# V projected in a phase of its own ahead of the attention, in place of inside every attention step

## The reference

```python
q, k, v = proj(x, Wq), proj(x, Wk), proj(x, Wv)      # x (8, 512, 1024), W (1024, 1024), 16 heads of 64
q = q * min(cond_1, 4.0)                             # one factor per batch
scores = einsum('bhqd,bhkd->bhqk', q, k) / 8, causal mask
attn = softmax(scores)
out = einsum('bhqk,bhkd->bhqd', attn, v)             # then back to (8, 512, 1024)
y = einsum('bsd,ed->bse', out, Wo)
result = x + absmax_int8(y) @ ternary(weight).T + bias
```

## Time and profile before

| what | value |
|---|---|
| runs | 2063.09 us median of 3 (2062.89 to 2063.57) |
| profiled execution | 2063.89 us |
| its span, first to last instruction | 2062.1 us |
| granted TensorE clock, mean | 0.999 of full |
| PE matmul busy | 2035.6 us, 99% |
| DVE, ACT, POOL busy | 1274.7, 1010.7, 803.8 us (62, 49, 39%) |
| DMA | 194.51 MB, mean 94 GB/s |

### The profile page before, as it was taken

How to read it: one execution, slowest core, us unless ns; L and a number is a source line. 1 busy time by engine, 2 the same in 40 slices (tenths; PEclk the granted TensorE clock), 3 DMA queues, 4 the chain that set the end, 5 groups by cost and what they waited for, 6 DMA issues and landing times.

```text
span 2062.1 us, 36378 instructions
## 1 busy us (share of the span) xinstructions
PE 2035.6 (99%) x11747; PEld 1725.0 (84%) x11778; DVE 1274.7 (62%) x3163; ACT 1010.7 (49%) x2383; POOL 803.8 (39%) x746
## 2 busy tenths in 40 slices
PE   8999999999999999999999999999999999999998
PEld 7888888888888888888888888888887777777775
DVE  5666666766666667666666766667766545455454
ACT  5656556655656566666565766656565000000000
POOL 3433333433333334344433433333334544444441
PEclk9999999999999999999999999999999999999999
DMA  4222223222222242222224223323223432333322
GB/s 164 72 73 89 92 71 138 77 78 72 71 72 71 79 140 72 72 71 71 72 89 155 73 98 115 121 93 93 92 72 104 137 122 92 112 101 104 109 98 75
DMA packets 85936, 194.51 MB, mean 94 GB/s; under 512 B 7392, under 2 KB 40160, under 8 KB 84320
## 3 DMA queue, kind: packets, MB, share of 16 engines
q1 hardware_dynamic: 85856, 193.50, 29.3%
HBM read 126.36 MB, written 33.55 MB: 78 GB/s over the span
## 4 chain that ended last, share of the span: by engine, by line
PE 48%; issue 30%; POOL 19%; ACT 1%; DVE 1%; POOLq 1%; DMA 0%; DVEq 0%; SPq 0%; ACTq 0%
PE proj_ps L170 18%; POOL prob L284 12%; PE s_ps L563 9%; PE proj_ps L563 8%; POOL parts L374 7%; PE o_ps L634 5%; PE t_ps L294 3%; PE o_ps L330 2%; PE s_ps L254 1%; PE s_ps L253 1%; PE t_ps L612 1%; ACT parts L370 0%; POOLq L283 0%; DMA w_raw<-wq 0%; ACT v_st L201 0%
## 5 line engine op out<-in xcount | busy, mean ns | idle before, releaser
L170 PE MATMUL proj_ps<-parts 128*128 128x512 f32 (+1 forms) x6144 | 1214.3, 345 | 10.1 <-DVE parts L374 10.1
L170 PEld LDWEIGHTS proj_ps<-parts 128*128 128x128 f32 x6144 | 929.9, 190 | 119.5 <-issue 10.1
L284 POOL TENSOR_TENSOR prob<-prob,row_inv 128x128 f32<-128x128 f32 (+3 forms) x512 | 393.4, 771 | 932.3 <-DVE row_inv L278 929.9
L265 DVE CUSTOM_DVE_ANT_0 prob<-s_ps,mask 128x128 f32<-128x128 f32 (+3 forms) x512 | 249.8, 488 | 340.3 <-PE t_ps L294 194.3
L308 ACT ACTIVATE pt_hi<-t_ps 128x128 fp32r<-128x128 f32 (+3 forms) x512 | 222.3, 434 | 434.7 <-PE t_ps L294 430.4
L272 ACT ACTIVATE prob<-prob,row_min 128x128 f32<-128x128 f32 (+3 forms) x512 | 286.3, 559 | 72.9 <-DVE row_min L265 66.9
L315 DVE TENSOR_TENSOR pt_lo<-t_ps,pt_hi 128x128 fp32r<-128x128 f32 (+3 forms) x512 | 249.5, 487 | 65.5 <-ACT pt_hi L308 59.9
L619 ACT ACTIVATE yt_q<-t_ps 128x1024 bf16<-128x1024 bf16 x32 | 32.8, 1025 | 428.0 <-PE t_ps L612 428.0
L294 PE MATMUL t_ps<-ident,prob 128*128 128x128 f32 x1280 | 227.7, 276 | 7.3 <-POOL prob L284 5.7
L374 POOL TENSOR_TENSOR parts<-x_raw,parts 128x512 fp32r<-128x512 f32 x128 | 203.1, 1607 | 51.5 <-ACT parts L370 51.5
L563 PE MATMUL proj_ps<-parts 128*128 128x512 f32 x768 | 186.2, 396 | 0.0
(11 more groups left out here) (65 smaller groups left out, 1902.9 us busy)
## 6 DMA issues: line engine op xcount, KB each, us to landing
x_raw<-xT SPq DMA_DIRECT2D x128, 512.0 KB, 5.5
k_sw<-k_st SPq DMA_DIRECT2D x128, 256.0 KB, 3.7
oT_scratch<-o_sum SPq DMA_DIRECT2D x64, 256.0 KB, 2.3
x_raw<-oT_scratch SPq DMA_DIRECT2D x32, 512.0 KB, 4.6
x_tile<-x SPq DMA_DIRECT2D x32, 512.0 KB, 5.2
out<-res SPq DMA_DIRECT2D x32, 512.0 KB, 3.1
w_raw<-wf SPq DMA_DIRECT2D x16, 512.0 KB, 5.6
w_raw<-wq SPq DMA_DIRECT2D x4, 1024.0 KB, 7.0
```

What stands on the lines that cost most here:

```text
L170: mm = pe.matmul(out, l, r, start=(k == 0 and i == 0), stop=(k == KT - 1 and i == 2))
L265: dve.tensor_tensor_reduce(prob[:, u % 4, 0:w], s_ps[u % 2][:, 0:w], mask[:, S - w:S], 1.0, -MASKED, ALU.add, ALU.min, row_min[:, u % 4:u ...
L284: pool.tensor_tensor(prob[:, u % 4, 0:w], prob[:, u % 4, 0:w], row_inv[:, u % 4:u % 4 + 1].broadcast_to([P, w]), ALU.mult).then_inc(norm_d ...
```

## The change

V leaves the attention. A new phase, ahead of it, computes V for all 4096 tokens and 1024 features and writes it, high and low part side by side, to a scratch tensor in HBM (33.5 MB). It works through 16 pairs of 128-token tiles. Pair 0 is computed plainly: 8 slices of 12 matmuls of 512 columns, 96 in all, while the weight (4 MB) arrives and is split. Pairs 1 to 15 use a scheme with 7 products of half-size blocks in place of 8 (Winograd's form of Strassen's): 7 products of 12 matmuls of 512 columns, 84 a pair. It needs four sums of weight quarters once (`wv_sums`, on DVE, of 128x2048 each), their splits, and for each pair four sums of x quarters (POOL), 7 splits of 128x512 (ACT and DVE), 4 copies from PSUM (ACT), 5 sums (DVE, one on POOL), 4 splits of the result (ACT and DVE) and 4 stores of 512 KB.

In the attention, groups gi 4 to 7 go, with their evacuations and the V weights' loads and splits. `v_st` still has one buffer. Each step loads its V in one DMA of 1 MB (chunks of 2 KB), which SP issues once the last PV of the step before has finished. The orders are written anew for the shorter steps: now units 0 to 4 (before: 0 to 7) get their scores in their own step and the rest in the next, T(0) to T(2) likewise; T(u) still follows S(u+2). The 32 J slices left lie mostly two between one S/T pair and the next. Loads, splits of weights and `Y` products are moved to match. Buffers move to make room: the V phase's tensors share SBUF with the attention's. The memsets of `pt_hi` and `pt_lo` ahead of the attention go.

```diff
-        groups = [("q", 0), ("k", 0), ("q", 1), ("k", 1)] + [("v", t) for t in range(QT)]
+        groups = [("q", 0), ("k", 0), ("q", 1), ("k", 1)]
...
         def times_v(pe, it, h):
 
             pe.wait_ge(pt_lo_done, it * UNITS + (h + 1) * QT)
-            if h == 0:
-                pe.wait_ge(const_ready, 4)
-                pe.wait_ge(proj_lo_done, (it + 1) * NEV)
+            pe.wait_ge(v_in, (it + 1) * 16)
             pe.wait_ge(o_sum_done[h % 2], it * NBLK + h // 2 + 1)
...
+        def load_v(sp, it, g, b):
+            if due(count := it * HG):
+                sp.wait_ge(pv_done, count)
+            sp.dma_start(v_st[:, :, :, :].rearrange("p t h d -> p t (h d)").bitcast(F32),
+                         v_scr[bass.ds(b, 1), :, :, g, :, :].rearrange("a t p h d -> p (a t) (h d)")).then_inc(v_in, 16)
...
+        def v_plain(pe):
+            for k in range(KT):
+                pe.wait_ge(wv_lo_done, 2 * k + 2)
+                if k % CH == 0:
+                    pe.wait_ge(xv_lo_done, 2 * (k // CH) + 2)
+                ks = slice(k % CH * P, (k % CH + 1) * P)
+                for j in range(2):
+                    c = B_PLAIN[k // CH][j]
+                    for i, a in enumerate((A11, A21_PLAIN) if k < CH else (A12, A22)):
+                        for m, (xp, wp) in enumerate(((1, 0), (0, 1), (0, 0))):
+                            mm = pe.matmul(plain_bank(j, i)[:, :], xv[:, c, xp, ks], wv_view(a, wp)[:, k % CH, :],
+                                           start=(k == 0 and m == 0), stop=(k == KT - 1 and m == 2))
...
+        def v_product(pe, n, c):
+            done = 4 * (n - 1)
+            pe.wait_ge(xv_lo_done, 4 + 7 * (n - 1) + c + 1)
+            if n == 1 and c in ws_lo_done:
+                pe.wait_ge(ws_lo_done[c], 1)
...
+            for k in range(CH):
+                ks = slice(k * P, (k + 1) * P)
+                for m, (xp, wp) in enumerate(((1, 0), (0, 1), (0, 0))):
+                    mm = pe.matmul(bank[:, :], xv[:, c, xp, ks], wv_view(c, wp)[:, k, :],
+                                   start=(k == 0 and m == 0 and c not in (S2, S3)), stop=(k == CH - 1 and m == 2),
+                                   skip_group_check=(c in (S2, S3)))
+            mm.then_inc(v_product_done, 1)
...
         @block.tensor
         def _(pe):
+            v_pe(pe)
             pe.wait_ge(const_ready, CONSTS)
             program(pe, pe_step)
```

More of the change, by code:

```diff
@@ L188, in halves @@
             return [(2 * blk, slice(0, DH), slice(DH, P)), (2 * blk + 1, slice(DH, P), slice(0, DH))]
-        def v_view(t, part):
-            return v_st[:, t, :, part, :]
         def evac_hi(act, it, gi):
@@ new lines, in adaln_ffn_kernel, with wv_view, wv_quad, xv_quad @@
+        v_lo_done = sem("v_lo_done")
+        v_stored = [sem(f"v_stored{i}") for i in range(2)]
+        def wv_view(c, part):
+            return (wv_first if c < 4 else wv_last)[:, c % 4, part, :].rearrange("p (k e) -> p k e", e=HALF)
+        def wv_quad(i, j):
+            return wv_raw[:, j * CH:(j + 1) * CH, i * HALF:(i + 1) * HALF]
+        def xv_quad(n, i, j):
+            return xv_raw[:, n % 2, j, i * CH * P:(i + 1) * CH * P]
+        V_TMP_A, V_TMP_U, V_TMP_R, V_TMP_P = range(4)
+        bank_x, bank_w, bank_z = o_ps, t_ps[0], t_ps[1]
@@ new lines, in wv_split @@
+        def wv_split(eng, k, low):
+            for i, c in enumerate((A11, A21_PLAIN) if k < CH else (A12, A22)):
+                raw = wv_raw[:, k, i * HALF:(i + 1) * HALF]
+                if low:
+                    eng.wait_ge(wv_hi_done, 2 * k + i + 1)
+                    eng.tensor_tensor(wv_view(c, 1)[:, k % CH, :], raw, wv_view(c, 0)[:, k % CH, :].bitcast(F32),
+                                      ALU.subtract).then_inc(wv_lo_done, 1)
+                else:
+                    eng.activation(wv_view(c, 0)[:, k % CH, :], raw, ACT.Copy).then_inc(wv_hi_done, 1)
@@ new lines, in adaln_ffn_kernel, with xv_split_plain @@
+        XV_PLACE = [(0, 0), (1, 1), (1, 0), (1, 1), (0, 0), (0, 1), (1, 0)]
+        def xv_split_plain(eng, i, j, low):
+            c = B_PLAIN[i][j]
+            n = 2 * i + j
+            if low:
+                eng.wait_ge(xv_hi_done, n + 1)
+                eng.tensor_tensor(xv[:, c, 1, :], xv_quad(0, i, j), xv[:, c, 0, :].bitcast(F32),
+                                  ALU.subtract).then_inc(xv_lo_done, 1)
+            else:
+                eng.wait_ge(xv_in[0], 32)
+                eng.activation(xv[:, c, 0, :], xv_quad(0, i, j), ACT.Copy).then_inc(xv_hi_done, 1)
@@ L682, in program, with v_pool @@
+        def v_pool(pool):
+            xv_sums(pool, 1)
+            ws_low(pool, S2)
+            ws_low(pool, S3)
+            for n in range(1, PAIRS):
+                xv_sums(pool, n + 1)
+                if n == PAIRS - 1:
+                    x_low(pool, 0, 1)
+                v_ur(pool, n)
+            for k in range(3, KT, 2):
+                x_low(pool, 0, k)
         def program(eng, step):
@@ L1157, in sp_step @@
                 load_wf(sp, KT + 2 * wf_part - 1)
-            if last and now:
-                load_wo(sp, 3)
-                load_wo(sp, 4)
-                load_wo(sp, 5)
-        CONSTS = 4 + 2 + 3 + 3
+        CONSTS = 2 + 3 + 3
         block = ctx.enter_context(nc.Block())
@@ L1222, in _ @@
         def _(dve):
[L1224 to L1226 removed]
+            v_dve(dve)
             dve.wait_ge(const_ready, CONSTS)
```

888 lines of the change are left out of this document (573 added, 315 removed).

## The result

The changed kernel takes **2130.84 us** (median of 4 runs, 2129.91 to 2132.53) against 2063.33 for the kernel before in the same runs: 1.0327 times as long, 95% interval 1.0309 to 1.0345, or +67.5 us. The forecast had the sign, and 2077.4; the time lies 17 us above its range. The profiled execution's span is 2130.5 us, 68.4 more than before's.

What follows compares the result with a forecast made beforehand. PE was taken as the bound everywhere, busy for 99% of the span. Terms -378.9 + 319.2 + 5 + 3 + 56 + 8 + 2 summed to +14.3 us, so 2077.4 us, with a range of 2018 to 2114.

Steps and rivals of the forecast that it cites:

- rival 2: At PV(0) in each step: V arrives late, PE waits 1.2 us, total 2114 us; chance 0.10.
- Rival 3: In the V phase: not PE-bound, a store or x sum late, 2 us a pair, total 2105; chance 0.10.
- Rival 1: In the attention steps: the order holds, T waits cost only 0.5 us a step, total 2022; chance 0.35.
- The steps become tight: +56: Attention steps without V: late T(1), T(4), T(5) cost net 1.8 us in 31 steps, +56 us (+6 to +95).
- 0.3 late: At T(4) in each step: behind ACT's V3, DVE's low part, L2 and I4, T(4) comes 0.3 us late.
- those 5.7 us of today are in the 36.9, so net 1.8: Attention steps: present normalisation waits, 5.7 us, already lie in the 36.9 us step, so 2.0 us of waits become net 1.8.
- 6.1 us: From S(u) to T(u), two slots: the chain had 6.1 us before, now 4.0 where no PV stands between.
- The swaps of k have some 1.3 us to spare: On SP behind V's load: k's swaps land with some 1.3 us to spare before S(0) and S(8).
- Cover is there for half: about 1.5 us in each of 7: Steps with weights or final weight work: half is covered, about 1.5 us in each of 7, +8 us (0 to +25).
- The start: Start of the V phase: first matmul at about 11 us, short waits for sums and splits, +5 us (0 to +18).
- Rival 4: Shared port of DVE and POOL: one engine held for the other, 1 us a step, total 2108; chance 0.03.
- 0.68 + 1.73 = 2.4: DVE's x low parts beside POOL: a whole-operation hold would give up to 2.4 us; the longest is 1.77.

Runs made afterwards that it cites:

- e1: Changed kernel with V loaded only in the first step, the other 31 loads of 1 MB left out; 2127.76 us, 1.0312 times the kernel before.
- e4: Changed kernel with DVE making the reciprocal of unit 1 and mask of unit 2 ahead of x's low part 0; 2126.68 us.
- e7: e5 with POOL's normalisation 3 ahead of x part 3, DVE's reciprocal 1 right behind V2, weights' splits moved out of the stretch; 2110.53 us.
- e13: e5 plus e2's early swap, a reordered start with sums' low parts on DVE, and POOL's normalisation 3 ahead of x's low part 3; 2098.58 us.
- e2: Changed kernel with SP issuing the first step's K swap ahead of the next step's x load (2 MB); 2123.83 us, 1.0293 times the kernel before.
- e5: Changed kernel with ACT, DVE and POOL reordered from T(14) to T(5), the chain ahead of evacuations and splits; 2093.39 us, 1.0144 times the kernel before.

## Why the prediction was wrong

**What held.** PE is what both kernels are about; the V matmuls went and the phase came at the price forecast (pairs 2 to 15 each 84 matmuls, 0.2268 us in place of 0.2354; the phase ends at 336.46, forecast 335 to 345). V's load is hidden: e1 shows it, and 1 MB lands after 5.3 us by the median where 8.5 were priced, so rival 2 falls. Rival 3 falls but for pair 1. Rival 1 falls: the order doesn't hold. The waits lie where the text put them: T(1) 0.74 late in place of 0.7, T(5) 0.86 in place of 1.0.

**Where the 54 us come from** (span +68.4, forecast +14.3), by PV(0) to PV(0):

| term | forecast | measured | off by |
|---|---|---|---|
| up to the first PV(0) (54.1 before, -11.8, +327.2) | 369.5 | 378.33 | +8.8 |
| plain steps, 31 x | 38.66 | 39.63 | +30.1 |
| weights and ternary steps, above plain | 8 | 17.3 | +9.3 |
| last interval, above plain (before 1.6 below, +2) | 0.4 | 4.4 | +4.0 |
| from the last PV(0) on (before 499.4) | 499.4 | 502.0 | +2.6 |

That is 54.8 against 54.1; the rest is rounding. The 2.6 at the end were not looked into: that part is the same in most of the runs and takes 500.7 to 504.3 us.

**The step that failed is "The steps become tight: +56".** The mechanism was right and its size was off: 2.77 us net a step in place of 1.8, 86 in place of 56. Two parts of it. First, T(4), forecast "0.3 late", measured 0.7, and T(0), of which nothing was said, 0.26. T(4)'s path was named rightly (ACT's V3, DVE's low part, L2 and I4) but not added up; by the rows it takes 3.7 us from the end of J(3,7), at about 450.7, to T(4), where PE's own work takes 3.0. The late points were worked out one by one from an engine that was thought on time when the stretch began; e4, e7 and e13 show that it isn't, because each engine's queue carries its delay to the next point. Second, "those 5.7 us of today are in the 36.9, so net 1.8" took off 0.2 a step. The stretches without a wait give 36.8, so nothing was to be taken off. The high end of the term, 3 a step (93 us in 31 steps, written as 95), did hold the measured value; with this miss alone the time would be about 2107, inside the range, and it lies outside because the other terms missed in the same direction. The comparison of "6.1 us" before with "4.0" now is uneven: 6.1 is an eighth of 48.70 and has PV's time in it, 4.0 has none; it is used in no sum.

**The swap.** "The swaps of k have some 1.3 us to spare" was worked out for a step that has one before it. In step 0 SP issues x's 2 MB first, and the swap was priced at its usual landing. The wait is 8.19 us; moving the swap leaves 1.85 of it and gives back 7 in all (e2). The same happens once more, late in the attention: 1.29 us in one step, behind V's load and 1 MB of the final weight.

**Weights and ternary.** "Cover is there for half: about 1.5 us in each of 7" failed. In a ternary step DVE is busy for 33.35 us in place of 28.87. The second of its two Q, with one operation at 1.67 us beside POOL, and PE's waits at T(0) and T(2), from the timeline:

```profile
1486.67 1.67 DVE L475 TENSOR_SCALAR wf_raw<-wf_raw 128x1024 f32<-128x1024 f32 x1
1488.37 0.70 DVE L477 TENSOR_SCALAR w_raw<-wf_raw 128x1024 bf16<-128x1024 f32 x1
...
1485.96 1.83 POOL L365 TENSOR_TENSOR parts<-x_raw,parts 128x512 fp32r<-128x512 f32 x1
...
1483.42 0.33 PE L283 MATMUL t_ps<-ident,prob 128*128 128x128 f32 x1 [1.30 <-POOL prob L273]
1490.10 0.55 PE L283 MATMUL t_ps<-ident,prob 128*128 128x128 f32 x3 [0.77 <-POOL prob L273]
```

I0 stands behind the first Q on DVE and I2 behind the second, so T(0) and T(2) wait on top of all the others: 3.1 us a step in place of 1.5, and 4.4 in the first of the four. Of the step ahead of these, 41.08, 1.3 is S(0)'s wait for the swap. This is read from the trace; no run took Q away. The weights' pair of steps, for its part, costs 0.7 (40.62 and 39.37 against twice 39.63), less than forecast; but in e4 and e5, where the plain step has fewer waits, the pair costs 5.0 and 4.4. The waits of the plain step had been their cover, as it seems; no run tests that by itself.

**The start.** First matmul at 13.8 in place of 11, and pair 1 takes 30.9 us in place of 19.1, 12 more where some 4 were forecast: 7.3 us of waits, and slow matmuls behind them. The quicker matmuls of pairs 2 to 15 made up for it, and two misses cancelled.

**Rival 4** had been given 0.03 because no row showed a whole operation held. In pair 1 two were: 5.03 and 5.05 us for splits of 0.69 beside POOL's 5.08 and 5.02. The price of x's parts in the steps was right, since the earlier trace rows are what they take with the holding in them, at most 1.78. The reason given against the rule was not: "0.68 + 1.73 = 2.4" adds a POOL length that itself has time held in it. POOL's operation alone takes 1.28, so a split held for all of it takes 1.8 or so, and 1.77 is such a split. All 96 DVE splits over 0.77 us in the kernel before end 0.55 us behind a POOL operation. At the start, where POOL's operations are four times as long, it was left out. The Trainium skill (SBUF — State Buffer, Who interferes with whom) says that the loser fully blocks; the traces agree with it, in pair 1 (5.05 us) as in the steps. The holding was in both kernels, so it was no rival to the steps' sum but a part of its prices; what was missing is its price at the start.

**What stays open.** Which of J's evacuations and the chain's own length makes the last 1.0 us was not separated, and no run took the normalisation off POOL. Nor was an order tried that puts the x splits in the first two stretches, which have no waits.

## What to carry to other kernels

When work is taken from the bounding engine, what counts is not the others' average load (DVE and ACT are busy for 73 and 71% of a step here) but the stretch in which their work is densest: add up each queue there from the point where it was last idle, and carry its delay on from one point to the next. A wait that one reordering removes is worth what is left after the next wait has grown; turn all engines' orders together, measure the whole step, and look again at the steps with extra work, whose cover was the wait. In a one-time start look at what the first small transfer stands behind.
